# A decoder layer on one core: the first head group of the first batch built in two halves, and its neighbours' projections, rotations and loads at other places

## What is computed

```python
def layer(x, ctx, w_atten, w_proj, ...):
    # x: (4, 512, 512)
    q, k, v = split(ln(x) @ w_atten.T, 3)       # 16 heads of 32 features
    q, k = rope(q), rope(k)                     # x0*cos - x1*sin, x1*cos + x0*sin
    att = softmax(causal(q @ k.T / sqrt(32)))
    x = x + (att @ v) @ w_proj.T
    x = x + cross_attention(ln(x), ctx)         # softmax over 512 context positions
    return x + experts(ln(x))                   # 8 experts, 2 per token, and a shared one
```

## Time and profile before

| | us |
|---|---|
| median of 3 runs | 1135.32 |
| lowest, highest | 1135.26, 1137.61 |
| the profiled execution, its own time | 1135.84 |
| its span, first to last instruction | 1134.1 |
| mean granted TensorE clock | 0.978 |

### The profile page before, as it was taken

The page is one execution under the profiler, slowest core; times in us unless marked ns, Lnnn a source line. Parts: engine busy times, 40 slices in busy tenths (PEclk is TensorE's granted clock), DMA queues, the critical chain, the costliest instruction groups (busy, mean ns, idle before and its releaser), DMA issues.

```text
span 1134.1 us, 17912 instructions
## 1 busy us (share of the span) xinstructions
PE 1048.3 (92%) x6128; PEld 750.5 (66%) x6128; DVE 601.2 (53%) x1592; ACT 483.0 (43%) x1265; POOL 178.4 (16%) x204
## 2 busy tenths in 40 slices
PE   6577799999999999899889999999999999999998
PEld 3244454564544646455455779988888898889997
DVE  3445555676467764676455355734444324444565
ACT  1154565564554655546472333124444424442221
POOL 2111111121011210112000000111111111112232
PEclk9888899999999999999999999999999999999999
DMA  6654445425163252432513102063443244423554
GB/s 189 130 99 57 56 57 75 56 29 76 48 110 48 34 75 54 75 41 35 115 38 105 28 20 75 28 239 137 151 151 128 98 151 152 153 71 121 149 173 152
DMA packets 57706, 107.03 MB, mean 94 GB/s; under 512 B 5728, under 2 KB 18528, under 8 KB 57632
## 3 DMA queue, kind: packets, MB, share of 16 engines
q1 hardware_dynamic: 52032, 87.72, 33.5%
q0 software_dynamic: 5600, 18.35, 5.7%
HBM read 59.66 MB, written 21.23 MB: 71 GB/s over the span
## 4 chain that ended last, share of the span: by engine, by line
PE 67%; DVE 11%; DMA 11%; issue 5%; ACT 2%; POOL 2%; SPq 2%; DVEq 0%; ACTq 0%; POOLq 0%
PE ps L1098 18%; PE ps L1108 10%; DMA ks<-rope_b 8%; PE ps L864 7%; PE ps L906 5%; PE ps L929 3%; PE ps L946 3%; PE ps L1004 3%; PE ps L883 3%; PE ps L895 3%; PE ps L1088 2%; DVE gu_lo L1394 2%; PE ps L966 1%; PE ps L1116 1%; DMA y_d<-y_sb 1%
## 5 line engine op out<-in xcount | busy, mean ns | idle before, releaser
L1245 DVE CUSTOM_DVE_ANT_0 probs<-ps,mask 128x128 f32<-128x128 f32 (+3 forms) x256 | 123.7, 487 | 139.6 <-PE ps L895 126.1
L663 ACT COPY probsT<-ps 128x128 f32<-128x128 f32 (+3 forms) x256 | 108.7, 425 | 191.8 <-PE ps L906 189.7
L895 PE MATMUL ps<-ks,qs 96*128 96x256 f32 (+2 forms) x256 | 149.2, 585 | 33.8 <-DMA ks<-rope_b 23.9
L655 ACT ACTIVATE probs<-probs,nb 128x128 f32<-128x128 f32 (+3 forms) x256 | 145.7, 569 | 33.6 <-DVE nb L1250 32.8
L864 PE MATMUL ps<-xnT,wa_sb 128*128 128x512 f32 x256 | 128.6, 617 | 3.6 <-DVE rope_b L1228 3.0
L906 PE MATMUL ps<-ident,probs 128*128 128x128 f32 x640 | 120.2, 287 | 0.1
L752 ACT ACTIVATE sg<-ps 128x352 f32<-128x352 f32 x69 | 32.0, 464 | 196.8 <-PE ps L1098 196.7
L1519 DVE TENSOR_TENSOR hidden<-sg,ps 128x352 f32<-128x352 f32 x69 | 35.9, 520 | 142.5 <-ACT sg L752 142.3
L895 PEld LDWEIGHTS ps<-ks,qs 96*128 96x128 f32 x256 | 50.7, 198 | 79.0 <-issue 36.4
L906 PEld LDWEIGHTS ps<-ident,probs 128*128 128x128 f32 x640 | 77.0, 144 | 33.7 <-issue 29.2
L556 POOL TENSOR_TENSOR rope_a<-rope_a,sin_sb 128x512 f32<-128x512 f32 x32 | 40.8, 1275 | 346.4 <-DVE rope_a L1227 346.4
(11 more groups left out here) (159 smaller groups left out, 1942.0 us busy)
## 6 DMA issues: line engine op xcount, KB each, us to landing
gu_raw<-in_we SPq DMA_DIRECT2D x10, 1408.0 KB, 6.8
y_d<-y_sb SPq DMA_DIRECT2D x37, 256.0 KB, 2.4
qs<-rope_b SPq DMA_DIRECT2D x32, 256.0 KB, 5.0
ks<-rope_b SPq DMA_DIRECT2D x32, 256.0 KB, 7.5
shared_x<-xn_d SPq DMA_DIRECT2D x32, 256.0 KB, 2.7
d_raw<-in_we SPq DMA_DIRECT2D x10, 512.0 KB, 7.6
qs<-rope_a SPq DMA_DIRECT2D x16, 256.0 KB, 7.2
ks<-rope_a SPq DMA_DIRECT2D x16, 256.0 KB, 8.4
```

Of the source, the lines that this page charges most:

```text
L655: nc.scalar.activation(pr, pr, ACT.Exp, bias=nb[:, n % 2, h:h + 1], scale=SCALE, accum_out=sums[:, n % 2, h:h + 1]).then_inc(exp_done, 1)
L663: nc.scalar.copy(probsT[n % 2][:, h, 0:w], ps[:, T_BANK + h % 2, 0:w]).then_inc(pT_done, 1)
L895: nc.tensor.matmul(ps[:, S_BANK + h % 2, 0:w], qs[:, G % 2, h, i * P:(i + 1) * P], ks[:, G % 2, h, 0:w], start=True, stop=True).then_inc(s ...
L1245: nc.vector.tensor_tensor_reduce(probs[n % TT][:, h, 0:w], ps[:, S_BANK + h % 2, 0:w], mask[:, TOKENS - w:], 1.0, LOWEST, ALU.add, ALU.max ...
```

## The change

The first group of the first batch (G = 0) is made in two halves of 256 tokens: statistics, root, scaling, transposes, projections (256 columns), rotation and stacking are each done for tiles 0 and 1 and then for tiles 2 and 3. The copies of a half move 128 KB each, in rows of 256 tokens (1 KB). The first half's copies count on a semaphore of their own, `stacked_first`, for which the first two steps' scores wait; the third step waits for the second half on `stacked`. The four half projections go to four banks.

SP's order is new: tiles 0 and 1, weights of group 0, tables, tiles 2 and 3, value weights, the first half's copies, then the two remaining parts of the query and key weights (PE still waits for both before its first scores), then the second half's copies. The x of batch 1 goes behind the copies of group 1, the later weights and the context of batch 0 behind those of group 2, the x of batch 2 behind those of group 3.

In all groups the copies of a high part are issued when the high part is made (`rope_high`), and only that of the low part waits for POOL (`rope_done`).

Value tile 0 of batch 0 stays in the prologue; tiles 1 to 3 go to places 0 to 1, 7 to 8 and 10 to 11. Projections and rotations of groups 1 to 4 have tables of their own; their keys are projected into other banks (`O_BANK` for group 1, `X_BANK` for 2 to 4), so that they need not wait for the queries' products. The values of batch 0 wait for the rotation products that free their banks. Lines that only count semaphores anew (`unit`) are left out, as are POOL's functions, which take a half and its columns in the same way as DVE's.

```diff
+EARLY_QUERIES = {1: (2, 2, 3, 3), 2: (-2, -2, -1, -1), 3: (-2, -2, -1, -1), 4: (45, 45, 46, 46)}
+EARLY_KEYS = {1: (4, 4, 5, 5), 2: (0, 0, 1, 1), 3: (0, 0, 1, 1), 4: (47, 47, 48, 48)}
+EARLY_RAW = {1: (4, 6), 2: (0, 2), 3: (0, 2), 4: (47, 49)}
+EARLY_SUM = {1: (6, 8), 2: (2, 4), 3: (2, 4), 4: (49, 51)}
+FIRST_VALUES = ((-1, -1, -1, -1), (0, 0, 1, 1), (7, 7, 8, 8), (10, 10, 11, 11))
+FIRST_VALUE_COPIES = (-1, 1, 9, 12)
...
-        FIRST_QK_BANKS = (QK_BANK, O_BANK)
-        FIRST_VALUE_BANKS = (T_BANK, T_BANK + 1, QK_BANK)
-        EARLY_VALUES = len(FIRST_VALUE_BANKS)
+        HALVES = (slice(0, TOKENS // 2), slice(TOKENS // 2, TOKENS))
+        FIRST_QK_BANKS = ((QK_BANK, O_BANK), (T_BANK, T_BANK + 1))
+        FIRST_VALUE_BANKS = (T_BANK, T_BANK + 1, QK_BANK, O_BANK)
+
+        def qk_bank(G, i):
+
+            if i and G <= GROUPS:
+                return O_BANK if G == 1 else X_BANK
+            return QK_BANK
...
-            def stack_part(G, i):
-
-                stacks, parts = ((qs, (rope_b, rope_b, rope_a)), (ks, (rope_b, rope_a, rope_b)))[i]
-                sp.wait_ge(rope_done, 2 * G + i + 1)
-                for j, part in enumerate(parts):
-                    sp.dma_start(stacks[j * HDIM:(j + 1) * HDIM, G % 2, :, :].bitcast(F32),
-                                 part[i][:]).then_inc(stacked, 16)
+            def stack_high(G, i, half=0, cols=slice(0, TOKENS), done=stacked):
+
+                sp.wait_ge(rope_high, unit(G, i, half) + 1)
+                for j in ((0, 1), (0, 2))[i]:
+                    sp.dma_start((qs, ks)[i][j * HDIM:(j + 1) * HDIM, G % 2, :, cols].bitcast(F32),
+                                 rope_b[i][:, cols]).then_inc(done, 16)
+
+            def stack_low(G, i, half=0, cols=slice(0, TOKENS), done=stacked):
+
+                j = (2, 1)[i]
+                sp.wait_ge(rope_done, unit(G, i, half) + 1)
+                sp.dma_start((qs, ks)[i][j * HDIM:(j + 1) * HDIM, G % 2, :, cols].bitcast(F32),
+                             rope_a[i][:, cols]).then_inc(done, 16)
...
+            for t in range(TT // 2):
                 sp.dma_start(acc[:, t, :], x_v[0][:, t, :]).then_inc(x_loaded[t], 16)
+            load_wa(0)
+            load_wa(1)
+            sp.dma_start(cos_sb[:], cosT).then_inc(tables_loaded, 16)
+            sp.dma_start(sin_sb[:], sinT).then_inc(tables_loaded, 16)
+            for t in range(TT // 2, TT):
+                sp.dma_start(acc[:, t, :], x_v[0][:, t, :]).then_inc(x_loaded[t], 16)
+            load_wa(2)
+            for half, done in enumerate((stacked_first, stacked)):
+                for i in range(2):
+                    stack_high(0, i, half, HALVES[half], done)
+                    stack_low(0, i, half, HALVES[half], done)
+                if half == 0:
+                    load_wa(3)
+                    load_wa(4)
...
+                if place == group_start(1) + EARLY_SUM[1][1]:
+                    load_x(1)
+                if place == group_start(2) + EARLY_SUM[2][1]:
...
+                    load_context(0)
+                if place == group_start(3) + EARLY_SUM[3][1]:
+                    load_x(2)
...
             def scores(n, h):
...
-                if i == 0 and h == 0:
+                if n == 0 and h == 0:
+                    pe.wait_ge(stacked_first, STACK)
+                if h == 0 and (i == 0 and G or n == 2):
                     pe.wait_ge(stacked, (G + 1) * STACK)
...
-            pe.wait_ge(norm1.copied, TT)
-            for i in range(2):
-                pe.wait_ge(wa_loaded[i], 16)
-                project_qk(0, i, range(CC), FIRST_QK_BANKS[i])
+            for half in range(2):
+                for t in (2 * half, 2 * half + 1):
+                    if half:
+                        pe.wait_ge(norm1.copied, t - 1)
+                    turn_tile(norm1, 0, t, X_BANK + t % 2)
+                pe.wait_ge(norm1.copied, 2 * half + 2)
+                for i in range(2):
+                    pe.wait_ge(wa_loaded[i], 16)
+                    project_qk(0, i, range(CC), FIRST_QK_BANKS[half][i], HALVES[half])
             pe.wait_ge(wa_loaded[2], 16)
-            for t, bank in enumerate(FIRST_VALUE_BANKS):
-                values(0, t, range(CC), bank)
+            values(0, 0, range(CC), FIRST_VALUE_BANKS[0])
             for loaded in wa_loaded[3:]:
                 pe.wait_ge(loaded, 16)
...
+            def rope_products(G, i, bank, half=0, cols=slice(0, TOKENS)):
+
+                raw, low, high = ps[:, bank, cols], rope_a[i][:, cols], rope_b[i][:, cols]
                 if G:
+                    dve.wait_ge(stacked_first, STACK)
                     dve.wait_ge(stacked, G * STACK)
...
+            first_stats(0)
+            for t in range(2):
                 scale(norm1, 0, 0, t)
+            first_stats(1)
             dve.wait_ge(tables_loaded, 32)
+            rope_products(0, 0, FIRST_QK_BANKS[0][0], 0, HALVES[0])
+            dve.wait_ge(norm1.root_made, 2)
+            for t in range(2, TT):
+                scale(norm1, 0, 0, t)
+            rope_products(0, 1, FIRST_QK_BANKS[0][1], 0, HALVES[0])
             for i in range(2):
-                rope_products(0, i, FIRST_QK_BANKS[i])
-                rope_add(0, i)
+                rope_add(0, i, 0, HALVES[0])
+            for i in range(2):
+                rope_products(0, i, FIRST_QK_BANKS[1][i], 1, HALVES[1])
+            for i in range(2):
+                rope_add(0, i, 1, HALVES[1])
```

More of the change, by code:

```diff
@@ L280, in group_start, with units_at @@
             return b * PLACES + (g - 1) * STEPS if g else (b - 1) * PLACES
-        def units_at(place, first_at, at):
-            return [(G, i) for G in range(1, ALL_GROUPS) for i, when in enumerate(at if G % GROUPS else first_at)
+        def units_at(place, early_at, first_at, at):
+            return [(G, i) for G in range(1, ALL_GROUPS)
+                    for i, when in enumerate(early_at[G] if G in early_at else at if G % GROUPS else first_at)
                     if group_start(G) + when == place]
@@ L570, in cross @@
                         root(norm3, p)
-            root(norm1, 0)
+            first_root(0)
+            first_root(1)
             pool.wait_ge(tables_loaded, 32)
-            for i in range(2):
-                times_sine(0, i)
-                low_of_sum(0, i)
+            for half in range(2):
+                times_sine(0, 0, half, HALVES[half])
+                times_sine(0, 1, half, HALVES[half])
+                low_of_sum(0, 0, half, HALVES[half])
+                low_of_sum(0, 1, half, HALVES[half])
             for place in range(DRAINED):
-                for G, i in units_at(place, FIRST_ROPE_RAW, ROPE_RAW):
+                for G, i in units_at(place, EARLY_RAW, FIRST_ROPE_RAW, ROPE_RAW):
                     times_sine(G, i)
-                for G, i in units_at(place, FIRST_ROPE_SUM, ROPE_SUM):
+                for G, i in units_at(place, EARLY_SUM, FIRST_ROPE_SUM, ROPE_SUM):
                     low_of_sum(G, i)
@@ L712, in _ @@
                 copy_first_turned(0, t)
-            for t, bank in enumerate(FIRST_VALUE_BANKS):
-                copy_values(0, t, bank)
             for place in range(DRAINED):
@@ L725, in _ @@
                         copy_inverse(n)
+                if place == 0:
+                    copy_values(0, 0, FIRST_VALUE_BANKS[0])
                 for b in range(BATCHES):
-                    for t in tiles_at(place, b * PLACES, VALUE_COPIES):
-                        if b or t >= EARLY_VALUES:
-                            copy_values(b, t, QK_BANK)
+                    for t in tiles_at(place, b * PLACES, value_places(b)[1]):
+                        copy_values(b, t, QK_BANK if b else FIRST_VALUE_BANKS[t])
                 for b in range(1, BATCHES):
@@ L856, in project_qk @@
                     if i:
[L857 removed]
+                        before = (G - 1, 1) if bank == X_BANK else (0, 1) if bank == O_BANK else (G, 0)
+                        pe.wait_ge(rope_raw, 2 * unit(*before) + 2)
                     elif g == 0:
                         pe.wait_ge(norm1.copied, b * TT + TT)
+                    elif G == 1:
+                        pe.wait_ge(rope_raw, 2 * unit(0, 0) + 2)
                     else:
[L861 removed]
+                        pe.wait_ge(v_done, b * TT + (1, 3, 4)[g - 1])
                 for c in chunks:
                     col = i * DIM + g * P
[L864 removed]
+                    last = nc.tensor.matmul(ps[:, bank, cols], wa_sb[:, c, col:col + P], xnT[:, c, cols],
                                             start=(c == 0), stop=(c == CC - 1))
@@ L869, in values @@
             def values(b, t, chunks, bank=QK_BANK):
-                if 0 in chunks and bank == QK_BANK:
-                    if t == 0:
-                        pe.wait_ge(rope_raw, 2 * (2 * GROUPS * b + 2))
-                    elif b == 0 and t < EARLY_VALUES:
-                        pe.wait_ge(rope_raw, 2)
+                if 0 in chunks:
+                    if b == 0:
```

(12 more changed lines are left out.)

133 lines of the change are left out of this document (69 added, 64 removed).

## The result

The changed kernel takes 1130.64 us (median of 7 runs, 1124.65 to 1132.41), the kernel before 1135.73 on the same chip (1134.38 to 1141.03): ratio 0.9929, 95% interval 0.99 to 0.9957. So it is faster, but by 5 us in the medians (8 by the ratio, which compares means) where 29 were forecast. The profiled execution took 1132.41, the longest of the seven; its span is 1130.5, its mean clock 0.971.

A forecast was written before the change was run, and what follows sets the result against it. Before 140 us, PE was taken to be held mainly by stack copies (20.3 us of waits). Batch 1 27.8 sooner plus 1.4 for early high parts gave 29.2: 1106.6 profiled, 1106 as median; range 1101 to 1118.

The forecast's parts named there:

- First scores: Start of group 0: statistics of two tiles start the work, so scores begin at 28.2 us, 9.5 sooner.
- Half copies: First stack of group 0: six half copies cost by bytes, 6.2 us, and land at 23.9.
- rival A: First stack: a half copy costs as much as a full one, total 1112 us; chance 0.14.
- Group 0: From first scores at 28.2 us until its successor's copies land: group 1 starts at 60.4, 7.6 sooner.
- First issues: Groups 1 and 2: copies are first issued 9.3 us after a group's start, where it was 17.6 before.
- rivals B: Key chain keeps its length, first issue stays 17.6 us after a group's start; gain 15.3, total 1120 us; chance 0.08.
- rival C: Group 0's halves do not overlap; gain gone above 4.2 us a half copy, 1147 us one at a time; chance 0.04.
- High parts early: All groups: high parts issued 1.4 us earlier gain 1.4 at one later waiting start, between 0 and 3.7.
- Groups 1 and 2: Copies set the first at 23.7 us, PE the second at 26.4; group 2 at 84.1, group 3 at 110.5.
- Group 3: 25.78 less 1.8 moved projection, 1.6 cold, 1.6 wait behind VectorE: 20.8 us; batch 1 at 131.3, 27.8 sooner.
- rival D: Nothing gained: PE's waits only change their name, maxima instead of copies, total 1135 us; chance 0.02.
- two cold starts of 1.6 each that stay: Upper end of the range: these and 3 us more of maxima waits, added to rival A, reach 1118 us.

The follow-up runs named there:

- e4: e2 plus 15 needless projection matmuls for PE at places 2 to 6 of groups 1, 2 and 3; median 1123.84 us.
- e6: e2 with the projections and rotations of group 4 back at their places of before the change; median 1115.87 us.
- e2: Changed kernel with sums of groups 2 and 3 at places 3 and 7, not 2 and 4, group 4's at 50 and 54; median 1120.46 us.
- r1: The changed kernel run and traced once more, unaltered; median 1130.03 us.
- r2: e6 run and traced once more, unaltered; median 1115.24 us.
- r3: e2 run and traced once more, unaltered; median 1117.29 us.

## Why the prediction was wrong

**Right.** First scores: 28.2 forecast, 29.69 measured. Half copies cost by their bytes: from first issue to first scores 12.06 us against 12.5, and while they ran alone the engines moved 147 GB/s, more than full copies' 127:

```profile
22.00:23.00 1.00, 1.00 (x3) 0.38 (x2) 0.97 (x3) 0.00 (x0) 0.46 (x1) 1.00 1.17 147
...
26.00:27.00 1.00, 0.00 (x0) 0.00 (x0) 0.00 (x0) 0.00 (x0) 0.00 (x0) 1.00 1.07 372
```

That settles rival A: 128 KB at 147 GB/s are 0.9 us a copy. The Trainium skill (SBUF — State Buffer, The DMA setup-cost knee) has a fixed cost of roughly 2 us for every transfer; as a cost that adds up from copy to copy, as it was set against the change, these copies do not show it. The 1.5 us by which first scores missed lie ahead of the copies, whose first issue came at 17.63 instead of 15.7: the first sixteen half projections took 5.64 us instead of 16 × 0.24 = 3.8, though the granted clock was 1.00; the second sixteen took 3.72. Why the first were slow wasn't tried. Group 0: 32.2 forecast, 31.79 measured. First issues come 8.8 and 9.1 us after the starts of groups 1 and 2 (forecast 9.3, though its terms add to 9.2), from SP's timeline:

```profile
46.97 1.19 SPq L443 DMA_DIRECT2D qs<-rope_b  x2
...
70.28 1.19 SPq L443 DMA_DIRECT2D qs<-rope_b  x2
...
99.06 1.20 SPq L443 DMA_DIRECT2D qs<-rope_b  x2
```

So the copies of groups 2 and 3 landed before they were wanted, and rivals B and C did not come. (By its own chain rival C's limit is 4.0 us a half copy and not 4.2.) High parts early won less than the 1.4 us of the forecast at the one later start that waits, within its 0 to 3.7: the wait fell by 1.0 from the 3.68 of the earlier trace rows, and the start comes 32.5 us behind the one before it instead of 33.1. In the change:

```profile
539.88 0.58 PE L961 MATMUL ps<-ks,qs 96*128 96x256 f32 x1 [2.66 <-DMA ks<-rope_a]
```

**The step that failed** is in "Groups 1 and 2" and "Group 3": a group was given the longer of two times, that of the copies and "PE needs in group 1 27.82, less 1.6 cold, 1.0 wait on a product, 3.6 for the value tile that left: 21.6", "26.4" and "25.78 - 5.0 = 20.8". As PE's need these are not too low: 68.8 us in all, where e4 shows 62.2 at full clock. But PE's need is not a group's length. A third time was left out: the masks on VectorE, one behind the other, with a rotation of some 6 us put among the first five places. It was costed only as a link of the chain to the copies ("a mask and its wait, 0.9"), not as a delay of every mask behind it. That is close to rival D, maxima in place of copies, which had 0.02, though waits on maxima took over only 3.8 of the 13.2 us that waits on copies and weights lost.

Of the 17.2 us by which batch 1 missed its forecast, 1.1 stand at the start of group 1. In groups 1 and 2 there are 10.2: e6, at about the same clock (0.87 and 0.88 against 0.88 and 0.84), is 5.9 shorter, which is put down to the order; e2, at 1.00, another 3.6, put down to the clock. The second traces (r1, r2, r3) give 8.5 and 2.1, so the split is a rough one. What is left, 0.7 in e2 and 2.1 in r3, is what the forecast misses with the sums apart; in group 1 it hits by luck, as said. Group 3 missed by 6.0, and in every version by 4.4 or more. Of the 5.0 taken off 25.78, the moved projection (1.8) won nothing by e6, the cold start (1.6) stayed, with a mean clock of 0.87 against 0.88, and the wait behind VectorE (1.6) became one of 0.8, with another of 3.1 for a maximum beside it.

**A term that was mis-sized:** the clock. The forecast put "two cold starts of 1.6 each that stay and 3 us more of maxima waits" into its range. The waits grew by 3.8, near that. But behind them the clock was low for some 7 us at a time, and groups 1 to 3 ran at 0.84 to 0.88 in the mean.

**Behind batch 1** the forecast assumed that PE runs as before, less the 1.4. Of the 25.8 us between the 1106.6 of the forecast and the profiled 1132.41, 17.2 stand ahead of batch 1 and 8.4 behind it (0.2 lie outside the span). "Rest" in the table is 975.0 for the kernel before and 971 to 984 for the versions, with the same instructions. The change lost 7.0 there, r1 0.5, e6 won 4.0. A stretch of group 12 in the change and then in e2, at the same distance from the group's start:

```profile
435.00:438.00 3.00, 3.00 (x31) 2.26 (x32) 1.18 (x6) 1.04 (x4) 0.00 (x0) 0.83 0.00 0
438.00:441.00 3.00, 3.00 (x12) 1.97 (x12) 0.00 (x0) 0.87 (x3) 0.00 (x0) 0.60 0.00 0
```

```profile
427.19:430.19 3.00, 3.00 (x33) 2.11 (x33) 1.18 (x6) 1.18 (x5) 0.00 (x0) 1.00 0.00 0
430.19:433.19 3.00, 3.00 (x26) 2.76 (x25) 0.43 (x2) 1.49 (x6) 0.00 (x0) 1.00 0.00 0
```

PE is full in both, with the same instructions in the same order, and in one the clock falls to half for some 3 us. The runs of one kernel spread by up to 13 us (e2), and their clocks with them: 0.986 in e2's fastest run, 0.973 in its slowest. So the clock takes part of what batch 1 gained. What decides it stays open.

## What to carry to other kernels

When a wait on one engine is taken away, list what every other engine must do in the same places, and take the longest of all, not what is left of the bound engine's own time. Work moved earlier in a software pipeline should go where the pacing engine has slack: here a few numbers in a table, the sums of a rotation one and three places later, were worth more than the whole change had brought. Ask of each stall what clock stands behind it, and look at a second execution before a gain of under 1% is put down to an order.
